# Sorting both halves of a top-1 masked feed forward by expert, in place of dense products over expert groups for the first half, in a two-layer gated kernel on one core

## The chip, the cores and the metric

The program runs on one core of a Trainium2 chip. The metric is the device time in microseconds of one execution; a comparison goes by the median of several runs. The engines of the core are named as the profile names them: PE is TensorE (PEld its weight loads), DVE is VectorE, ACT is ScalarE, POOL is GpSimd, SP is SyncE, which here only issues DMAs.

## What is computed

The input x is 4 x 256 x 256 float32, that is 1024 tokens of 256 features. Four updates of x follow each other; g are gates read from inputs.

```python
x = x + tanh(g_xattn[0]) * attn0(layernorm(x), ctx)        # sim of x, row norm, softmax
x = x + tanh(g_ffn[0])   * ffn0(layernorm(x))              # ternary weight, 32 masks, top 1 of 32
x = x + tanh(g_xattn[1]) * adj1(ctx, layernorm(x))         # top 76 of 256 per row, symmetric part
x = x + tanh(g_ffn[1])   * ffn1(layernorm(x))              # 64 experts, top 8, plus a shared one

def ffn0(x, weight, scale, expert_masks, router_w):        # masks: 32 x 256 x 256
    probs = softmax(x @ router_w.T)
    top1_w, top1_idx = max(probs), argmax(probs)
    w = clip(round(weight / 0.5), -1, 1) * scale[:, None]
    return (x @ (w * expert_masks[top1_idx]).T) * top1_w   # per token
```

## The kernel before

The 1024 tokens are 8 tiles of 128 rows (T = 8), four to a half (HT = 4). X holds the running x, XN its normalised rows, SIM the scores of the second attention, Z scratch. Every engine has its own list of instructions, written out by hand in the order in which it runs; semaphores hold an engine where it needs another's result, and whatever is behind such a wait on that engine waits too.

**The first feed forward.** POOL loads the 32 masks in eight pieces into `m16` (upper half of `gu16`), DVE multiplies each piece by the ternary weight (`mask_weights`, L1643). The two halves of the tokens take different ways. *First half, dense:* `choose(0)` finds each token's expert, `sort_rows` and PE's `group_rows` spread a tile's rows over four groups of eight experts, and PE's `dense(i, ...)` (L1000) multiplies each group with every mask position, 16 products of 16 matmuls; DVE (`dense_rows`, L1468 to L1474), ACT (`started`, `scaled`) and POOL (`add_parts`, `add_rows`) weight the results with `c_mem` and add them up. *Second half, sorted:* `choose(1)`, then PE's `ranks`, `owners`, `owners_of` and DVE's `assign_spares`, `assign_owners`, `assign_slots`, `set_owners` give each token a row number `slot` in a table of 12 x 128 rows, 32 rows per expert and 15 spare blocks for experts with more tokens. POOL's `scatter` (L443) writes the rows to the DRAM tensor `routed_rows`; SP's `load_spares` (L309) copies the weights of each spare block's expert; ACT loads the sorted rows (L719), PE transposes them (`routed_x`, L1018) and multiplies (`experts`, L1039) in six pieces; the results go by DRAM (`expert_rows`, L344) and POOL's `gather` (L451) back to token order.

**The thresholds.** The second attention needs the 76th largest of each row of SIM. DVE finds it with MAX8 and MATCH_REPLACE8 in turn, 19 steps for a tile; `find(n)` takes the next n steps wherever it stands in DVE's list. `adjacency(t)` applies it; `rows_affine`, `rows_sym`, `rows_mix` and `rows_normalise` (L1349) finish a half and hand it to the second feed forward.

**The second feed forward.** 32 pairs of experts and one shared step, for each half of the tokens: PE projects (`project`, L1115), ACT and DVE gate, POOL (`low_step`, L493) makes the low part of a split into two float16, PE multiplies down (L1142). A pair's float32 weights are loaded by SP into one of two stage buffers (`load_pair(q)`, stage q % 2, once pair q - 2 is split), rounded by ACT (`high_half`) and their remainder taken by POOL (`low_half`, L433 and L434). Pairs 0 to 9 are split before the steps begin, the others, four steps ahead, inside the loop of steps n = 2 to 32. At its head PE's list has `shared_step(0)` (L1101), one pair, `prep_wt(0)` (L1091), which needs the token weights, `first_weights` (L1127), the next pair. The token weights come from PE's logits by DVE's `top_find`, ACT's `top_rows` (L755) and DVE's `top_weigh`.

```python
            def load_pair(q):
                s = q % 2
                if q >= 2:
                    sp.wait_ge(lo_ready, q - 1)
```

## Time and profile before

| | us |
|---|---|
| median of 3 runs (407.02 to 409.56) | 408.67 |
| the profiled execution | 407.92 |
| its span on the core | 406.2 |
| PE busy | 384.1 (95%) |
| DVE busy | 283.1 (70%) |
| ACT busy | 184.0 (45%) |
| POOL busy | 162.4 (40%) |

The span runs from the first to the last instruction; what lies around it is 1.7 us. A matmul record's end is modelled, so PE's busy share is no measure of how well it is used. The granted clock of PE is a share of full speed (2.4 GHz): 0.50 is 1.2 GHz.

### The profile page before, as it was taken

The numbers are of one execution on the slowest core, as the hardware profiler recorded it, in microseconds if no ns is written. First come the engines' busy times: TensorE is split into PE (matmuls) and PEld (weight loads), VectorE is DVE, ScalarE is ACT, GpSimd is POOL, SyncE is SP. The second block draws the span as 40 slices with busy tenths as digits, with TensorE's granted clock in tenths as the row PEclk, the third lists the DMA queues.
The fourth block names the chain that finished last, engine by engine and source line by source line (L and its number), as shares of the span: only waits on it lengthen the run. The fifth ranks groups of instructions, "written<-read, shape, count | busy, mean of one in ns | idle before, by whom it ended". The sixth has DMA issues, their size and how long they took to land. (4 is left out here: it accounts for less than half of the span.)

```text
span 406.2 us, 7559 instructions
## 1 busy us (share of the span) xinstructions
PE 384.1 (95%) x2356; PEld 224.0 (55%) x2356; DVE 283.1 (70%) x728; ACT 184.0 (45%) x369; POOL 162.4 (40%) x182
## 2 busy tenths in 40 slices
PE   8989899999789699999999999969999999999995
PEld 2754355444366255656656566545665656656563
DVE  3989888999979568897984775447555545555454
ACT  3477966244166545455455545633333233332331
POOL 6924046849213556995999876220000000000000
PEclk9996999999989899999999999989999999999999
DMA  7799721493212333445456552014121211212211
GB/s 182 124 258 208 105 75 43 126 292 102 81 63 96 116 107 129 143 146 178 144 169 196 157 171 70 7 35 139 61 77 52 77 65 64 77 53 76 71 58 52
DMA packets 46521, 45.13 MB, mean 111 GB/s; under 512 B 6236, under 2 KB 37916, under 8 KB 46494
## 3 DMA queue, kind: packets, MB, share of 16 engines
q1 hardware_dynamic: 35822, 37.69, 30.1%
q0 software_dynamic: 8832, 5.24, 8.4%
q10 hardware_dynamic: 1840, 1.87, 1.6%
q8 instruction: 13, 0.21, 0.2%
q14 instruction: 14, 0.11, 0.1%
HBM read 42.03 MB, written 4.98 MB: 116 GB/s over the span
## 5 line engine op out<-in xcount | busy, mean ns | idle before, releaser
L1115 PE MATMUL bank<-early,gu 128*128 128x512 f16 x768 | 177.7, 381 | 1.3 <-DVE arena L1749 1.3
L1115 PEld LDWEIGHTS bank<-early,gu 128*128 128x128 f16 (+1 forms) x768 | 75.3, 98 | 80.7 <-issue 4.4
L539 ACT ACTIVATE arena<-arena 128x512 f16<-128x512 f32 (+1 forms) x66 | 41.5, 630 | 132.3 <-DVE arena L1765 130.9
L1142 PE MATMUL bank<-dp,arena 128*128 128x256 f16 (+1 forms) x768 | 94.7, 274 | 0.4 <-DVE arena L1775 0.4
L1142 PEld LDWEIGHTS bank<-dp,arena 128*128 128x128 f16 x768 | 75.4, 98 | 22.2 <-DVE arena L1775 0.7
L1749 DVE TENSOR_TENSOR arena<-arena,bank 128x512 f32<-128x512 f32 x64 | 43.9, 686 | 53.5 <-PE bank L1115 38.9
L1000 PE MATMUL bank<-gu,arena 128*128 128x512 f16 x256 | 57.6, 379 | 1.7 <-ACT arena L539 1.7
L493 POOL TENSOR_TENSOR arena<-arena 128x512 f16<-128x512 f32 (+1 forms) x33 | 38.7, 1173 | 39.6 <-ACT arena L539 39.6
L1765 DVE TENSOR_TENSOR arena<-arena,early 128x512 f32<-128x512 f32 x64 | 45.7, 714 | 7.2 <-DVE arena L1749 2.7
L769 ACT ACTIVATE arena<-bank 128x512 f32<-128x512 f32 (+1 forms) x66 | 38.7, 587 | 16.5 <-PE bank L1115 16.5
L433 POOL TENSOR_TENSOR gu<-stage,gu 128x512 f16<-128x512 f32 x32 | 38.4, 1202 | 8.6 <-ACT dp L539 8.6
L1000 PEld LDWEIGHTS bank<-gu,arena 128*128 128x128 f16 x256 | 24.7, 98 | 30.5 <-issue 2.5
L1775 DVE TENSOR_TENSOR arena<-arena 128x512 f16<-128x512 f32 (+1 forms) x33 | 22.8, 692 | 24.8 <-ACT arena L539 24.8
L1272 DVE MAX8 t<-work 128x8 f32<-128x256 f32 x72 | 30.6, 425 | 2.0
L434 POOL TENSOR_TENSOR dp<-stage,dp 128x256 f16<-128x256 f32 x32 | 28.7, 897 | 0.0
L1277 DVE MATCH_REPLACE8 work<-t,work 128x256 f32<-128x256 f32 x64 | 26.1, 408 | 0.0
L426 POOL TENSOR_TENSOR rstd<-var_in,minus_half 128x4 f32<-128x4 f32 x8 | 8.3, 1044 | 40.2 <-DVE var_in L1313 29.4
L539 ACT ACTIVATE arena<-bank 128x512 f16<-128x512 f32 (+2 forms) x28 | 15.6, 590 | 14.5 <-PE bank L1039 8.8
L539 ACT ACTIVATE gu<-stage 128x512 f16<-128x512 f32 x32 | 19.7, 617 | 3.3 <-DMA stage<-in_dp_t 3.2
L827 PE MATMUL bank<-ones 128*128 128x512 f16 x45 | 15.3, 511 | 1.1 <-DVE ones L1647 1.1
L1299 DVE BATCH_NORM_STATS2 bn<-X 128x6 f32<-128x256 f32 x32 | 11.8, 412 | 5.4 <-DMA X<-in_x 5.3
L420 POOL DMA_DIRECT2D gu<-in_masks_t x16 | 12.2, 768 | 3.3 <-DMA X<-in_x 3.3
(199 smaller groups left out, 357.3 us busy)
## 6 DMA issues: line engine op xcount, KB each, us to landing
early<-token_weights SPq DMA_DIRECT2D x126, 128.0 KB, 2.9
stage<-in_gu_t SPq DMA_DIRECT2D x32, 256.0 KB, 2.7
gu<-in_masks_t POOLq DMA_DIRECT2D x16, 256.0 KB, 24.1
stage<-in_dp_t SPq DMA_DIRECT2D x32, 128.0 KB, 3.1
dp<-gu SPq DMA_DIRECT2D x15, 128.0 KB, 2.4
routed_rows<-arena SPq DMA_DIRECT2D x1, 1536.0 KB, 17.8
arena<-routed_rows ACTq DMA_DIRECT2D x4, 384.0 KB, 5.1
expert_rows<-arena SPq DMA_DIRECT2D x6, 256.0 KB, 2.1
```

Source lines behind the costliest of these rows:

```text
L433: nc.gpsimd.tensor_tensor(gu16[:, q, 1, :, :], stage_gu[s], gu16[:, q, 0, :, :], ALU.subtract)
L434: nc.gpsimd.tensor_tensor(dp16[:, q, 1, :], stage_dn[s], dp16[:, q, 0, :], ALU.subtract).then_inc(lo_ready, 1)
L493: nc.gpsimd.tensor_tensor(inter16[0:m, s, 1, :], inter[0:m, s, :], inter16[0:m, s, 0, :], ALU.subtract).then_inc(ilo_ready, 1)
L539: return nc.scalar.activation(dst, src, ACT.Copy, scale=scale)
L769: nc.scalar.activation(silu[0:m, s, :], ps_gate[s][0:m, :], ACT.Silu).then_inc(silu_ready, 1)
L1000: last = mm(dst[:, :], xg[:, k, s, c, g * P:(g + 1) * P], m16[:, c, g * MB + 2 * bp:g * MB + 2 * bp + 2, :].rearrange("p e o -> p (e o)"), ...
L1115: last = mm(dst[:, :], w, x16[:, h, b, c, :], start=(k == 0), stop=(k == 3 * C - 1))
L1142: last = mm(dst, inter16[0:m, s, a, k * P:(k + 1) * P], w, start=(q is None and j == 0 and k % 2 == 0), stop=True, skip_group_check=True)
L1272: last = steps(v.max(t8[:, t, :], src))
L1277: last = steps(v.match_replace(work[:, :], t8[:, t, :], src, NEG))
L1749: v.tensor_tensor(gated[0:m, s, :], silu[0:m, s, :], up, ALU.mult).then_inc(gated_ready, 1)
L1765: v.tensor_tensor(inter[0:m, s, :], gated[0:m, s, :], row, ALU.mult).then_inc(inter_ready, 1)
```

## The change

Both halves of the tokens go the sorted way. `sort_rows`, `members`, `group_rows`, `dense`, `dense_rows`, `started`, `scaled` and `add_parts` are gone. The masks are stored and multiplied expert by expert. There are two sets of spare weights, two `slot` columns, two `expert_rows` tensors, two places for transposed rows; `routed_rows` is used twice. ACT stores the expert results instead of SP; POOL loads the second half's sorted rows. Pairs 0 to 7 are split before the loop of steps, pair 8 in step 4. The diff, cut to what is spoken of:

```diff
+        rows16 = arena[:, 0:4096].rearrange("p (k s n) -> p k s n", k=T, s=2)
+        xs16 = [xs16_0, late[:, 0:2 * ROWS * D].rearrange("p (k n) -> p k n", k=ROWS)]
 # SP
-            for q in range(2, 6):
+            load_pair(2)
+            load_pair(3)
+            load_spares(0)
+            load_pair(4)
+            load_pair(5)
+            load_spares(1)
+            for q in range(6, 8):
                 load_pair(q)
-            load_spares(0, 6)
...
-                if 4 <= n < PAIRS - 6:
+                if 2 <= n < PAIRS - 6:
                     load_pair(6 + n)
 # POOL
+            def load_rows():
+                pool.wait_ge(row_out, 16 * T)
+                pool.wait_ge(sim1_copied, 4)
+                for j in range(3):
+                    nc.gpsimd.dma_start(xs16[1][:, 4 * j:4 * j + 4, :], rows_v[:, 4 * j:4 * j + 4, :]
+                                        ).then_inc(xs_in[1][j], 16)
             rsqrt(1, HT)
+            low_half(0)
             rsqrt(2, HT)
+            low_half(1)
             for t in range(HT):
                 low_rows(t)
+            scatter(0)
+            low_half(2)
+            low_half(3)
...
             for t in range(HT, T):
                 low_rows(t)
-            low_half(2)
-            low_half(3)
-            scatter()
+            scatter(1)
+            load_rows()
+            gather(0)
+            rsqrt(4, HT)
             low_half(4)
-            low_half(5)
...
+            rsqrt(5, HT)
+            for q in range(5, 8):
+                low_half(q)
+            gather(1)
...
-                if n < 2 + HT:
-                    add_rows(n + 2)
-                elif n + 4 < PAIRS:
+                if 4 <= n < 4 + HT:
+                    add_rows(n)
+                if 4 <= n < PAIRS - 4:
                     low_half(n + 4)
 # ACT
             prep_rows(0)
-            expert_rows(PIECES - 1)
-            high_half(8)
-            high_half(9)
+            expert_rows(1, 5)
+            store_rows(1, 5)
+            for q in range(5, 8):
+                high_half(q)
             top_rows(0)
 # PE
+            sim1(1, 0, 1)
+            keep_busy(4, bank[0][:, :])
+            ranks(0)
+            keep_busy(2, bank[0][:, :])
+            owners(0)
+            keep_busy(2, bank[0][:, :])
+            owners_of(0)
+            keep_busy(36, bank[0][:, :])
+            routed_x(0, 0)
+            routed_x(0, 1)
+            experts(0, 0)
+            routed_x(0, 2)
+            experts(0, 1)
+            routed_x(0, 3)
+            router_x((2, 3))
+            experts(0, 2)
+            routed_x(0, 4)
             router(1)
...
+            routed_x(1, 4)
             symmetric(0, 0)
+            symmetric(0, 1)
+            experts(1, 3)
+            routed_x(1, 5)
+            experts(1, 4)
             prep_x3t(0)
-            experts(PIECES - 1)
+            experts(1, 5)
 # DVE
+            def rows_take(t):
+                dve.wait_ge(late_in, 16 * 4)
+                dve.wait_ge(y_in[t], 16)
                 steps.need(rows_mark[0])
+                m = steps(v.scalar_tensor_tensor(Z[:, t, :], Z[:, t, :], wtop[:, t:t + 1], scale_sb[:, :],
+                                                 ALU.mult, ALU.mult))
+                steps.need(m)
+                m = steps(v.tensor_tensor(X[:, t, :], X[:, t, :], Z[:, t, :], ALU.add))
+                steps.need(m)
+                m = steps(moments(X[:, t, :], t))
+                steps.need(m)
+                rows_mark[0] = steps(v.bn_aggr(mv[:, t, :], bn[:, t, :]))
+            find(6)
             choose(1)
+            find(2)
+            assign_spares(1)
...
+            thresholds(HT * need_of - used[0] - 8)
+            rows_take(0)
+            thresholds(2)
...
+            rows_take(3)
+            rows_ask(0)
+            find(2)
             rows_affine(0)
```

**DVE, right behind `choose(0)`.** Before: `grp` is the group of a token, `gu<-ident,grp` the spreading matrices, `picked` and `c_mem` the weights of the group members.

```order
L1427 TENSOR_TENSOR oh<-iota,idxf 128x128 [waits dve_step]
L1434 TENSOR_REDUCE grp<-oh 128x16 [waits dve_step]
L1440 TENSOR_TENSOR gu<-ident,grp 128x512 [waits dve_step]
L1440 TENSOR_TENSOR gu<-ident,grp 128x512
L1446 RECIPROCAL tiny<-tiny 128x4 [waits exp0_ready]
L1448 TENSOR_SCALAR tiny<-tiny,tg 128x4 [waits dve_step]
L1450 TENSOR_TENSOR picked<-oh,tiny 128x128 [waits dve_step]
L1453 TENSOR_REDUCE c_mem<-picked 128x32 [waits dve_step]
L1440 TENSOR_TENSOR gu<-ident,grp 128x512 x2
```

In the changed kernel the same place holds two finder steps and the ranking of the first half, which waits for PE.

```order
L1361 TENSOR_TENSOR oh<-iota,idxf 128x128 [waits dve_step]
L1206 MAX t<-work 128x8 [waits dve_step]
L1211 MATCH_REPLACE work<-t,work 128x256 [waits dve_step]
L1367 TENSOR_SCALAR spares<-full_at,bank 32x15 [waits rank_ready]
L1368 TENSOR_TENSOR picked<-oh,bank 128x128
L1371 TENSOR_REDUCE n_spare<-spares 32x1 [waits dve_step]
L1374 TENSOR_SCALAR n_spare<-ones,n_spare 32x128 [waits dve_step]
L1206 MAX t<-work 128x8 [waits dve_step]
L1380 TENSOR_TENSOR shifted<-shift_e,bank 128x32 [waits prior_ready]
```

What spread the rows over groups has gone; waits for `rank_ready`, `prior_ready` and `owner_ready`, which stood only behind `choose(1)`, now stand behind both.

**ACT, at the head of the second feed forward.** Before: the last expert results (L539 `arena<-bank`), pairs 8 and 9, then `top_rows(0)`.

```order
L539 ACTIVATE arena<-bank 128x512 [waits y_ready]
L539 ACTIVATE gu<-stage 128x512 [waits stage_in0]
L539 ACTIVATE dp<-stage 128x256
L539 ACTIVATE gu<-stage 128x512 [waits stage_in1]
L539 ACTIVATE dp<-stage 128x256
L755 ACTIVATE Z<-lg,tiny 128x64 [waits top_ready]
```

In the changed kernel a store is issued there, and the pairs are 5, 6 and 7.

```order
L506 ACTIVATE arena<-bank 128x512 [waits y_ready]
L641 DMA expert_rows<-arena 128x2x256 [waits y_copied]
L506 ACTIVATE gu<-stage 128x512 [waits stage_in1]
L506 ACTIVATE dp<-stage 128x256
L506 ACTIVATE gu<-stage 128x512 [waits stage_in0]
L506 ACTIVATE dp<-stage 128x256
L506 ACTIVATE gu<-stage 128x512 [waits stage_in1]
L506 ACTIVATE dp<-stage 128x256
L725 ACTIVATE Z<-lg,tiny 128x64 [waits top_ready]
```

Three pairs instead of two stand ahead of `top_rows(0)`, and the first and the third of them use the same stage buffer.

## Rows read from the trace of the kernel before

**Rows 1.** The chain that ended last: start us, us, what (one step of 66).
```profile
281.72 2.70 PE bank L1115 x12
284.42 1.31 PE bank L1142 x12
```

**Rows 2.** Timeline of PE, head of the second feed forward: start us, us, engine line op.
```profile
129.55 1.46 PE L1101 MATMUL bank<-early,shared 128*128 128x512 f16 x6
130.84 2.75 PE L1115 MATMUL bank<-early,gu 128*128 128x512 f16 x12
134.71 0.65 PE L1091 MATMUL bank<-ident,Z 128*65 128x128 f32 x4 [1.11 <-DVE Z L1635]
139.43 4.26 PE L1115 MATMUL bank<-early,gu 128*128 128x512 f16 x12 [1.26 <-DVE arena L1749]
```

**Rows 3.** Timeline of ACT, the same place.
```profile
128.23 0.58 ACT L539 ACTIVATE arena<-bank 128x512 f32<-128x512 f32 x1
131.58 0.35 ACT L755 ACTIVATE Z<-lg,tiny 128x64 f32<-128x64 f32 x1 [1.12 <-DVE tiny L1617]
```

**Rows 4.** Timeline of DVE, from the first half's choice to its hand-over.
```profile
38.17 0.29 DVE L1434 TENSOR_REDUCE grp<-oh 128x16 f16<-128x128 f16 x1
43.93 0.43 DVE L1382 CUSTOM_DVE_ANT_0 Z<-Z,beta_sb 128x256 f32<-128x256 f32 x1
77.53 3.68 DVE L1526 TENSOR_SCALAR tiny<-tiny,tg 128x4 f32<-128x4 f32 x1
87.84 0.43 DVE L1272 MAX8 t<-work 128x8 f32<-128x256 f32 x1
112.10 0.43 DVE L1540 TENSOR_TENSOR Z<-Z,scale_sb 128x256 f32<-128x256 f32 x1
118.78 1.90 DVE L1591 SCALAR_TENSOR_TENSOR X<-SIM,k_mix,Z 128x256 f32<-128x256 f32 x4 [1.89 <-ACT Z L581]
123.84 1.36 DVE L1349 TENSOR_SCALAR XN<-X,mv,rstd 128x256 f32<-128x256 f32 x4
```

**Rows 5.** Groups by line, ten of 17 dense sums: busy us, mean ns | idle.
```profile
L1474 DVE SCALAR_TENSOR_TENSOR Z<-bank,c_mem,Z 128x256 f32<-128x256 f32 x10 | 4.7, 472 | 0.3 <-ACT Z L539 0.2
```

**Rows 6.** Timeline of DVE, the sorted half's ranking, first and last.
```profile
66.78 1.04 DVE L1481 TENSOR_SCALAR spares<-full_at,bank 32x15 f32<-32x15 f32 x1 [0.39 <-PE bank L954]
71.93 0.17 DVE L1519 COPY place<-idxf 128x4 f32<-128x4 f32 x1
```

**Rows 7.** Timelines of POOL and ACT's queue, scatter and load of the sorted rows.
```profile
71.72 1.10 POOL L443 DMA_INDIRECT routed_rows<-gu,slot  x1 [1.56 <-DVE slot L1510]
79.09 2.23 ACTq L719 DMA_DIRECT2D arena<-routed_rows  x4
```

**Rows 8.** Line L719, then line L420 (the masks): time from issue to landing.
```profile
DMA to landing us min/median/max: 3.2/5.1/7.7
...
DMA to landing us min/median/max: 10.8/24.1/28.4
```

**Rows 9.** Timeline of SP's queue, the spare weights.
```profile
88.77 11.74 SPq L309 DMA_DIRECT2D dp<-gu  x9
```

**Rows 10.** The page, DMA issues of a pair: KB each, median us to landing.
```profile
stage<-in_gu_t SPq DMA_DIRECT2D x32, 256.0 KB, 2.7
stage<-in_dp_t SPq DMA_DIRECT2D x32, 128.0 KB, 3.1
```

**Rows 11.** Timeline of POOL: a split at the head, a step's split later.
```profile
129.71 1.16 POOL L433 TENSOR_TENSOR gu<-stage,gu 128x512 f16<-128x512 f32 x1 [6.02 <-ACT dp L539]
130.82 0.67 POOL L434 TENSOR_TENSOR dp<-stage,dp 128x256 f16<-128x256 f32 x1
165.98 1.16 POOL L493 TENSOR_TENSOR arena<-arena 128x512 f16<-128x512 f32 x1 [0.28 <-ACT arena L539]
```

**Rows 12.** Windows: length, busy us of PE, PEld, DVE, ACT, POOL, granted clock, DMA.
```profile
36.00:38.00 2.00, 2.00 (x6) 0.76 (x5) 1.86 (x16) 2.00 (x5) 0.67 (x1) 0.50 1.45 196
140.00:142.00 2.00, 2.00 (x7) 0.64 (x5) 1.08 (x2) 1.23 (x2) 0.71 (x1) 0.50 0.60 200
```

More of the change, by code:

```diff
@@ L720, in _ @@
[L720 to L733 removed]
+            routed_rows(1, 0)
+            routed_rows(1, 1)
@@ L1207, in _ @@
-            for p in range(PIECES - 1):
-                if p == 1:
-                    symmetric(0, 1)
-                experts(p)
-                if p + 2 < PIECES:
-                    routed_x(p + 2)
-            pe.wait_ge(dense_free, len(OWN))
-            keep_busy(12, bank[7][:, :])
+            sim1(1, 0, 1)
[5 more added lines that the diff above has]
+            owners_of(0)
@@ new lines, in _ @@
+            keep_busy(36, bank[0][:, :])
[8 more added lines that the diff above has]
+            routed_x(0, 4)
+            router(1)
+            experts(0, 3, 0)
+            ranks(1)
+            experts(0, 3, 1)
+            routed_x(0, 5)
+            owners(1)
+            experts(0, 4, 0)
+            owners_of(1)
@@ L1215, in _ @@
+            experts(0, 4, 1)
+            experts(0, 5)
+            keep_busy(8, bank[0][:, :])
+            routed_x(1, 0)
+            routed_x(1, 1)
+            experts(1, 0)
+            routed_x(1, 2)
+            experts(1, 1)
+            routed_x(1, 3)
+            experts(1, 2)
+            routed_x(1, 4)
+            symmetric(0, 0)
+            symmetric(0, 1)
+            experts(1, 3)
+            routed_x(1, 5)
+            experts(1, 4)
             prep_x3t(0)
-            experts(PIECES - 1)
+            experts(1, 5)
```

599 lines of the change are left out of this document (210 added, 389 removed).

## The prediction

> **What bounds the kernel now.** The chain that ended last comes first: from 267 us on it is PE almost without a gap, a projection of 2.7 us and a down product of 1.3 us, about 3.9 us a step [rows 1]. There are 66 such steps and no part of the change makes one shorter. So the time is the moment at which the steps get going, plus a constant. PE's timeline around that moment is next [rows 2]: the shared step starts at 129.55, the first pair ends at 133.6, then PE waits for the token weights (134.71) and for the first gated rows (139.43). From there it does not stop. PE's 95% in the page says nothing here; what counts is who is last before 129.55 and who between 133.6 and 139.43.
>
> Before 129.55 it is DVE. It hands the first half over at 123.84 [rows 4], the reader sees finder steps right up to it, and from 38.17 to 123.84 its 85.7 us have few gaps. Between 133.6 and 139.43 it is a round: DVE's `top_find`, ACT's `top_rows` at 131.58 (ACT had waited 1.12 us for it), DVE, PE at 134.71, ACT, DVE, PE [rows 2, 3].
>
> **The dense products (removed).** 256 matmuls leave PE. They lie ahead of DVE's end and their removal shortens nothing by itself: PE already waits for DVE there. What counts is what leaves DVE.
>
> **DVE's list, by difference.** Removed: spreading and member weights, everything from 38.17 to 43.93, 5.8 us [rows 4]; 17 dense sums of 0.47 us, 8.0 us [rows 5]; the wait of 1.9 us for `mix_rows`, which in the changed kernel no longer stands behind expert rows [rows 4]; and 3.4 of the 3.68 us of L1526, a four-element operation that sat beside POOL's splits [rows 4], as the changed place sits beside a scatter. Added: a second ranking; from 66.78 to 72.10 one took 5.3 us with two sums and two finder steps in it, so 3.4 us [rows 5, 6]; four `rows_take` of 1.6 us each (the row at 112.10 starts such a sequence of four operations, here 0.4 each) in place of one of them and three half ones, 3.2 us; two finder steps more before the hand-over and `weights_of_rows(0)`, 1.4 us, a finder step being 0.43 busy and 0.5 with its gap [rows 4]. Sum: -5.8 - 8.0 - 1.9 - 3.4 + 3.4 + 3.2 + 1.4 = -11.1 us.
>
> **DVE's new waits.** (a) The ranking of the first half waits for PE, which has eight float32 products and four fillers ahead of it, at the 1.2 GHz (0.50) that was granted at 36 to 38 us [rows 12]. DVE arrives at 38.2 and two finder steps, 39.2; by an estimate of 6 us for PE's twelve matmuls from 35.5 on, the counts arrive at 41.5: 2.3 us. (b) `choose(1)` waits for the second half's logits, and these now stand in PE's list behind four `routed_x` and three `experts`, which wait for the scattered rows. The slots are there at 41.5 and a ranking of 3.4, 44.9; scatter to first load took 7.4 us (71.72 to 79.09), beside mask products rather 8 [rows 7]; the load lands 3.2 to 5.1 later [rows 8], so 57. Then ACT and PE take turns (a copy of 1.0, one of 0.6 and a store issue of 0.45 a piece, two transposes of x that wait for each other's copy), with PE at 1.2 GHz in part: about 13.5 us, logits at 70.5. DVE gets there at about 66, an estimate from its list (the spare owners, twelve mask products, the second half's softmax and its 13 finder steps, some 21 us of work behind 44.9): 4.5 us. Both ends: no wait at all, or 12 us if PE stays slow throughout. I take 6.8, as the pieces are spaced by ACT in the rows of before too. Hand-over: -11.1 + 6.8 = -4.3 us, at 119.5.
>
> What else must be ready by then: the second half's slots at about 77.5, rows loaded from 85 on, and fifteen spare weights at 1.3 us [rows 9], from 79 to 99, landed by 102. PE wants them behind `symmetric(0, *)`, which waits for the fourth threshold at about 109. So these are hidden with 7 to 10 us to spare.
>
> **The head of the second feed forward.** Before, ACT went from the last expert rows (end 128.81) through pairs 8 and 9, long loaded, to `top_rows` at 131.58: 2.8 us with 1.1 of waiting in it [rows 3]. In the changed list three pairs, 5, 6, 7, stand there, and pair 7 can't be loaded before pair 5 is split, which begins only there. So: store issue 0.5, rounding of pair 5 0.8 (130.46 - 128.81 for two), POOL's split 1.8 [rows 11], issue of the second transfer 0.45 later and landing 3.1 [rows 10], rounding of pair 7 0.8: 7.5 to 7.8 us instead of 2.8. Everything behind `top_rows` (token weights, ACT's silu, the next pair on PE) is later by +4.9 us. Nothing covers it: `top_rows` was already what PE's 134.71 hung on. The bounds: +4.3 if the landing is 2.7, +7 if the queues are busy.
>
> **The clock.** Before, the pair at 139.43 took 4.26 us against 2.75, and the granted clock was 0.50, 1.2 GHz, at 140 to 142 [rows 2, 12], after PE had been mostly idle from 133.6. In the changed kernel this hole grows from 1.1 us to about 6 and the clock will fall earlier, so that the small matmuls of `prep_wt` and `first_weights` (some 3 us, on the path) run at 1.2 GHz too. I take +1.0 (0 to 3). *TensorE: Matmul & The Clock Gate* of the Trainium skill, in HAM oscillation, says that gaps in PE's work bring the lower clock back; by this rule, the trace agrees.
>
> **POOL in steps 4 to 7.** There `add_rows` (two operations, 1.6 us) now comes with a split. At 165.98 POOL had 0.28 us of waiting in a step of 3.6 [rows 11], so it falls behind by about 1 us a step, 4 in all; the low part is used two steps later, 7.8 us [rows 1], and most of that is free. +0.5 (0 to 4). Pair 8 comes four steps ahead of its use, as pair 10 did.
>
> *GPSIMD Engine Reference* of the Trainium skill (Specifications) says that GpSimd and VectorE contend for SBUF interfaces where VectorE runs in a two-port mode or with two SBUF inputs. The row at 77.53 agrees. The mask products have two SBUF inputs and now meet a scatter; by this rule they could be longer. The sum would then be a few tenths higher, no more, as masks and scatter overlap for 7 us only.
>
> **Sum.** -4.3 + 4.9 + 1.0 + 0.5 = +2.1 us. Against the profiled execution (407.92, span 406.2) that is 410.0; this execution was 0.75 under the median, so the median goes from 408.67 to about **410.8**.
>
> **The rivals.**
> *The forecast:* DVE's gain is real, about 4 us, and the stage buffer at the head eats it. Chance 0.48.
> *Faster (0.16):* DVE loses almost nothing to its new waits. Then the hand-over is 11 us earlier: 408.67 - 11.1 + 4.9 + 0.5 = 403. It decides from a gain at the hand-over above 10 us, as less than that leaves under 4 us behind the head. For it speaks that finder steps fill the list between the waits; against it, that `choose(1)` is bound to PE and ACT by program order.
> *Slower, the second half's rows come late (0.16):* POOL loads them through its own queue, and that queue's plain loads, the masks, took 10.8 to 28.4 us to land [rows 8]. Rows scattered by 85, six pieces of 2.4 us: last rows at 99 + landing, against 124.5 by DVE. It decides from a landing above 25 us; at 28.4 the time is 414. Against it: the masks were sixteen transfers on busy engines, here there are three.
> *Slower, POOL doesn't keep up (0.12):* if the buffer of two steps is used up by other things (mix rows, tanh), the 4 us of lag are paid: 414.5.
> *The rest (0.08):* PE slow through the first half's pieces, waits of 12 us: 416.
>
> **The range.** The cases give 403 to 416; with the bounds of the unknown costs 404 to 418 holds 8 in 10. About 1% (4 us) is what a measurement tells from no change: below 404.6 0.18, between 0.50, above 412.8 0.32.
>
> **What would show it.** The changed profile has: the DVE line of `normalise` near 119.5; DVE waiting 3 to 6 us for the logits' bank; ACT waiting 3 to 5 us for DMA `stage` right ahead of `top_rows`; PE waiting 5 to 7 us ahead of `prep_wt`; the second pair on PE near 141, and 3.9 us a step from there. A wait of ACT for `stage` under 1 us would make the head's term wrong; a hand-over before 114 or after 124 would make DVE's sum wrong; PE waits for `ilo_ready` in steps 5 to 10 would speak for POOL.

## The result, and the profile after

The changed kernel took 413.66 us (median of four runs) beside 409.12 for the kernel before: ratio 1.0123, 95% interval 1.0077 to 1.0169. It is slower by 1.2%, some 5 us. Predicted were 410.8 us, 404 to 418.

The executions of one kernel already differ in their first 20 us, and that shifts all that follows: DVE's first request for a root, an early mark, stands at 19.60 us in the profile of before and anywhere from 19.1 to 26.2 in those of the changed kernel and its variants. The inputs are not the reason, for DVE's first operation on x starts at 5.2 to 5.8 us in all of them; PE's first float32 products are what takes longer, here in the second execution of the changed kernel and in the first:
```profile
5.45 1.93 PE L807 MATMUL bank<-early,wk_sb 65*64 65x512 f32 x4
```
```profile
5.50 3.68 PE L807 MATMUL bank<-early,wk_sb 65*64 65x512 f32 x4
```
The first execution, the slowest of the four with 420.7 us, is slow by this alone: its mark stands 6.4 us later, and behind the mark it is no longer than the second. The profile read here is that second execution (414.78 us, span 412.9), in which the mark stands at 19.72, so its times can be laid beside those of before as they are. In the tables every run's times are shifted so that its mark stands at 19.70. *Hand-over* is the first row of `normalise`, *2nd pair* and *3rd pair* are projections of the second feed forward, *31st* the one ahead of `prep_wt(1)`.

| us | hand-over | shared step | `prep_wt` | 2nd pair | 3rd pair | 31st | end |
|---|---|---|---|---|---|---|---|
| before | 123.94 | 129.65 | 134.81 | 139.53 | 145.13 | 261.72 | 406.3 |
| after | 119.03 | 125.95 | 134.72 | 140.03 | 145.03 | 266.53 | 412.9 |
| after, first execution | 119.06 | 125.39 | 135.14 | 140.71 | 146.42 | 266.99 | 412.3 |

From column to column: the hand-over is 4.9 us earlier; from there to `prep_wt` it is 15.7 us for 10.9, so 4.8 are lost, and at the third pair both kernels stand at the same moment (in the first execution the changed one stands 1.3 later). Then, in 28 steps that the forecast had counted at 0.5 us, 4.9 us are lost, 4.0 in the first execution. Seven of the eight traces with this order of work in the steps have 4.0 to 4.2, so 4.0 is the better figure. Another 1.8 (0.7) lie at and behind the second half's preparation. That is no more than scatter: from the 31st projection to the end it is 144.6 to 146.4 us in the traces of all kernels here, and 146.4 in one that has the old kernel's steps (*before, with its share* in the last table).

The way from the hand-over to the shared step is itself no firm figure: it is 6.3 to 8.0 us in traces of kernels whose lists are alike there, while `prep_wt` comes 15.6 to 16.1 us behind the hand-over in all that have the changed kernel's pairs 5, 6 and 7 at the head.

DVE, timeline (start us, us, engine, line, operation; in brackets the idle time before it and who ended it), the places that answer to [rows 4, 6]:
```profile
41.67 0.23 DVE L1367 TENSOR_SCALAR spares<-full_at,bank 32x15 f32<-32x15 f32 x1 [1.42 <-PE bank L928]
44.83 11.07 DVE L1524 TENSOR_TENSOR gu<-gu,tern 128x1024 f16<-128x1024 f16 x12
57.60 0.23 DVE L1414 TENSOR_SCALAR tiny<-tiny,tg 128x4 f32<-128x4 f32 x1
70.70 0.29 DVE L1349 COPY lg<-bank 128x128 f32<-128x128 f32 x1 [2.79 <-PE bank L911]
111.17 1.14 DVE L1462 TENSOR_SCALAR mix<-rstd,k_mix 128x4 f32<-128x4 f32 x1 [0.31 <-POOL rstd L399]
119.05 1.36 DVE L1283 TENSOR_SCALAR XN<-X,mv,rstd 128x256 f32<-128x256 f32 x4
```
The two new waits are there, 1.42 us for the ranks and 2.79 for the logits. `weights_of_rows` takes 0.23 us where it took 3.68 [rows 4]. But twelve mask products take 11.07 us, which the kernel before did in 7.5. The line's own summary says why (durations in ns, smallest, median, largest):
```profile
L1524 DVE TENSOR_TENSOR gu<-gu,tern x16: 677/683/4328, 21.4 to 55.2; 128x1024 f16<-128x1024 f16 x16
```
One product out of sixteen took 4.3 us. It starts at 50.98, and POOL's timeline has at that moment the last scatter and then the two splits of pairs 2 and 3 without a pause:
```profile
50.98 4.33 DVE L1524 TENSOR_TENSOR gu<-gu,tern 128x1024 f16<-128x1024 f16 x1
...
50.26 0.96 POOL L420 DMA_INDIRECT routed_rows<-arena,slot  x1 [0.30 <-issue]
51.25 1.16 POOL L406 TENSOR_TENSOR gu<-stage,gu 128x512 f16<-128x512 f32 x1
52.35 0.67 POOL L407 TENSOR_TENSOR dp<-stage,dp 128x256 f16<-128x256 f32 x1
52.98 1.15 POOL L406 TENSOR_TENSOR gu<-stage,gu 128x512 f16<-128x512 f32 x1
54.09 0.66 POOL L407 TENSOR_TENSOR dp<-stage,dp 128x256 f16<-128x256 f32 x1
```
The product ends at 55.3, half a microsecond behind the last of them. The 3.4 us that [rows 4] shows on L1526 have not gone, they have moved. The affine at 111.17, too, lies beside a split: 1.14 us for its first operation, which takes 0.23 in the kernel before, and 0.59 for the second, 0.16 there.

PE and ACT at the head of the second feed forward, timelines, answering to [rows 2, 3]:
```profile
119.83 1.97 PE L1009 MATMUL bank<-ident,XN 128*128 128x128 f32 x8 [7.02 <-DVE XN L1283]
125.97 1.46 PE L1036 MATMUL bank<-early,shared 128*128 128x512 f16 x6
134.74 0.86 PE L1026 MATMUL bank<-ident,Z 128*65 128x128 f32 x4 [4.72 <-DVE Z L1516]
136.28 1.97 PE L1062 MATMUL bank<-early,ident 65*64 65x512 f32 x2 [0.68 <-ACT early L506]
138.18 2.08 PE L1062 MATMUL bank<-early,pick 65*128 65x512 f32 x2
...
124.72 0.63 ACT L506 ACTIVATE gu<-stage 128x512 f16<-128x512 f32 x1 [0.44 <-ACT arena L506]
130.48 0.63 ACT L506 ACTIVATE gu<-stage 128x512 f16<-128x512 f32 x1 [4.00 <-DMA stage<-in_dp_t]
131.32 0.33 ACT L725 ACTIVATE Z<-lg,tiny 128x64 f32<-128x64 f32 x1
```
ACT waits 4.00 us for pair 7's transfer, PE 4.72 us ahead of `prep_wt`, and what follows runs mostly at the lower of the two clocks, 0.59 in the mean (windows; the seventh figure after the window is the granted clock):
```profile
134.00:140.00 6.00, 4.58 (x8) 1.36 (x9) 1.85 (x6) 3.54 (x5) 3.30 (x4) 0.59 0.40 114
```
And PE's timeline of the steps. In the profile of before no projection or down product waits between the second pair and `prep_wt(1)`; here four do, 3.6 us together:
```profile
180.66 2.75 PE L1050 MATMUL bank<-early,gu 128*128 128x512 f16 x12 [0.33 <-DVE arena L1630]
188.09 1.48 PE L1077 MATMUL bank<-dp,arena 128*128 128x256 f16 x12 [0.69 <-POOL arena L465]
198.68 2.75 PE L1050 MATMUL bank<-early,gu 128*128 128x512 f16 x12 [1.22 <-DVE arena L1630]
204.19 2.75 PE L1050 MATMUL bank<-early,gu 128*128 128x512 f16 x12 [1.37 <-DVE arena L1630]
```

### The profile page after: what moved, and what is told of

Read it like the earlier page. It is cut to its first block and busy times, and to the rows that moved or that the text cites. A ratio compares the mean times of both kernels' runs of the same rounds, so it can differ in the third digit from the quotient of the medians.

```text
span 418.8 us, 7576 instructions
## 1 busy us (share of the span) xinstructions
PE 363.3 (87%) x2360; PEld 217.8 (52%) x2360; DVE 284.0 (68%) x723; ACT 179.0 (43%) x350; POOL 158.4 (38%) x175
## 3 DMA queue, kind: packets, MB, share of 16 engines
q0 software_dynamic: 9648, 7.87, 10.1%
## 5 line engine op out<-in xcount | busy, mean ns | idle before, releaser
L1646 DVE TENSOR_TENSOR arena<-arena,early 128x512 f32<-128x512 f32 x64 | 48.8, 763 | 7.2 <-DVE arena L1630 2.7
L739 ACT ACTIVATE arena<-bank 128x512 f32<-128x512 f32 (+1 forms) x66 | 38.7, 587 | 17.1 <-PE bank L1050 17.1
L798 PE MATMUL bank<-ones 128*128 128x512 f16 x70 | 22.6, 485 | 1.1 <-DVE ones L1528 1.1
L506 ACT ACTIVATE gu<-stage 128x512 f16<-128x512 f32 x32 | 19.7, 616 | 5.4 <-DMA stage<-in_dp_t 4.4
L506 ACT ACTIVATE gu<-bank 128x1024 f16<-128x1024 f16 x12 | 12.0, 1016 | 9.7 <-PE bank L954 9.4
L1233 DVE BATCH_NORM_STATS2 bn<-X 128x6 f32<-128x256 f32 x32 | 11.8, 414 | 4.8 <-DMA X<-in_x 4.5
L506 ACT ACTIVATE arena<-bank 128x512 f32<-128x512 f32 (+1 forms) x18 | 10.7, 593 | 9.8 <-PE bank L978 6.5
L978 PE MATMUL bank<-gu 128*32 128x256 f16 x256 | 11.9, 343 | 3.2 <-ACT gu L506 3.2
L798 PEld LDWEIGHTS bank<-ones 128*128 128x128 f16 x70 | 7.5, 116 | 13.0 <-issue 7.8
```

Of the source, the lines that this page charges most:

```text
L506: return nc.scalar.activation(dst, src, ACT.Copy, scale=scale)
L739: nc.scalar.activation(silu[0:m, s, :], ps_gate[s][0:m, :], ACT.Silu).then_inc(silu_ready, 1)
L798: mm(dst.rearrange("p (a b) -> p a b", a=4), ones16[:, :], ones16[:, None, :].to_broadcast([P, 4, P]), start=True, stop=True)
L1646: v.tensor_tensor(inter[0:m, s, :], gated[0:m, s, :], row, ALU.mult).then_inc(inter_ready, 1)
```

## Experiments

Theory at this point: four separate causes, (1) the stage buffer at the head, (2) POOL and DVE late in the steps, (3) one DVE product held by POOL's splits, (4) DVE's meeting with PE and ACT at the second half's logits. The rivals are that one of them covers for another, or that the second half's rows set the end anyway. Ratios are to the kernel before, measured beside each kernel on the same chip. The moments in the tables are shifted as above.

### The changed kernel again

> The changed kernel once more, unchanged, as the base for the three beside it: about 412.9 us. In the trace: the last mask product of DVE that lies beside POOL's splits of pairs 2 and 3 stretched to 4.4 us where the others take 0.6; DVE waits about 3.5 us for the second half's logits; hand-over (normalise) near 118.5 us; ACT waits about 4.4 us for stage ahead of top_rows; PE waits about 5.7 us ahead of prep_wt; some 4 us lost by PE between steps 10 and 16.

Measured: 418.4 us median of four runs that scatter from 414.8 to 420.9, ratio 1.025 (1.017 to 1.032), above the first measurement. The profile is the one shown above, and each expected figure is near: the long product 4.3 us, the wait for the logits 2.8, the hand-over 119.05, the waits of ACT and PE 4.0 and 4.7, and 4.9 us lost from the third pair to the 31st. Because runs of one kernel can differ by as much as the edits are worth, the following verdicts go by the moments in the traces, one trace a kernel. The times alone would not carry them: beside these four runs the next edits would be worth 5 to 7 us each, beside the first measurement 0 to 2.

### Pair 5 early (cause 1)

```diff
 ACT              high_half(4)
+                 high_half(5)
                  routed_rows(1, 0)
 ...
-                 for q in range(5, 8): high_half(q)
+                 for q in range(6, 8): high_half(q)
                  top_rows(0)
 POOL             low_half(4)
+                 low_half(5)
                  rsqrt(5, HT)
-                 for q in range(5, 8): low_half(q)
+                 for q in range(6, 8): low_half(q)
```

> Pair 5 is rounded and split right behind pair 4, among the expert rows of the second half, so pair 7's transfer is issued ten microseconds before it is wanted. If the stage buffer is what the head pays (theory): ACT's wait of 4.4 us goes, top_rows and prep_wt come 4.8 us earlier, the hole in PE falls from 5.7 to about 1 us, so prep_wt and first_weights run at 2.4 GHz again (-1.9 us), in all -4.8 to -6.7 us, 406 to 408 us. Rival (the round between DVE, ACT and PE is bound by something else that would end just as late, or the steps take the gain back because POOL lags anyway): within 1 us of the base.

Measured: 411.75 us, ratio 1.009 (1.004 to 1.014).

| us | hand-over | shared step | `prep_wt` | 2nd pair | 3rd pair | 31st | end |
|---|---|---|---|---|---|---|---|
| after | 119.03 | 125.95 | 134.72 | 140.03 | 145.03 | 266.53 | 412.9 |
| pair 5 early | 120.56 | 127.34 | 132.24 | 136.96 | 142.38 | 262.99 | 407.9 |

From the shared step to `prep_wt` 4.9 us instead of 8.8 (before: 5.2). PE and ACT of this kernel, timelines:
```profile
134.17 0.65 PE L1028 MATMUL bank<-ident,Z 128*65 128x128 f32 x4 [0.85 <-DVE Z L1518]
135.50 1.07 PE L1064 MATMUL bank<-early,ident 65*64 65x512 f32 x2 [0.68 <-ACT early L507]
138.89 4.08 PE L1052 MATMUL bank<-early,gu 128*128 128x512 f16 x12 [1.26 <-DVE arena L1632]
...
131.02 0.35 ACT L727 ACTIVATE Z<-lg,tiny 128x64 f32<-128x64 f32 x1 [1.10 <-DVE tiny L1500]
```
ACT's wait for `stage` is gone, it waits for DVE again as in [rows 3]. The buffer costs 3.9 us, and the smaller hole gives the higher clock back to `prep_wt` and `first_weights` (0.65 and 1.07 us where they took 0.86 and 1.97), while the second pair is slow as before. The loss in the steps is untouched (120.6 us from the third pair to the 31st against 116.6 before). The theory holds for the head: from the hand-over to `prep_wt` 11.7 us instead of 15.7, to the third pair 21.8 instead of 26.0 (before: 21.2). The time doesn't follow in full, 411.75 where 406 to 408 were expected. A part was paid back at once: the hand-over is 1.5 us later. The logits were already 0.8 us late, and at the affine pair 5's split now holds a further four-element operation (1.19 us for 0.16).

### `add_rows` out of the splits' steps, then the old places for the mixing work (cause 2)

```diff
 ACT, loop        weigh_rows: tiles 4, 5 at n == 2 (was 3), tiles 6, 7 at n == 3 (was 5)
 POOL, loop
-                 if 4 <= n < 4 + HT: add_rows(n)
+                 if 2 <= n < 4: add_rows(2 * n); add_rows(2 * n + 1)
```

> POOL's add_rows of tiles 4 to 7 go two each to steps 2 and 3, where no pair is split, with ACT's scaling of those rows at steps 2 and 3. If POOL's lag in steps 4 to 7 is what costs PE its 4 us between steps 10 and 16 (theory): those waits shrink to under 1 us in sum, time -3 to -4, about 409 us. Rival (the loss comes from mix_rows and tanh_rows on ACT or from DVE's own extra work in these steps, POOL is only near it): within 1 us of the base, and the waits of PE stay.

The second kernel has this and besides:

```diff
 DVE, loop
-                 rows_stats at n = 7..10, rows_ask at 10, rows_affine at 13
+                 rows_stats at n = 5..8,  rows_ask at 8,  rows_affine at 11
 POOL, loop       rsqrt(6) at n == 8 (was 10)
 ACT, loop        tanh_rows(1) at n == 4 (was 6), mix_rows(1) at 12 (was 14)
```

> add_rows two each in steps 2 and 3, as before, and besides DVE's, POOL's and ACT's mixing work of the second half (statistics, their root, affine, mix) two steps earlier, where the kernel before has it. With add_rows alone PE kept one wait of 1.4 us, behind mix_rows at step 14, and lost 2.0 us from step 2 to step 30 against 4 to 5. Theory: the rest is DVE's: steps 9 and 10 now hold four finder steps and the statistics, and step 13 an affine with an adjacency; at the old places PE waits nowhere from step 2 to 30, as in the kernel before: a further -1.5 to -2. Rival (the rest is mix_rows on ACT itself, wherever it stands): the wait of 1.4 us moves to step 12 and stays.

Measured: 411.98 us, ratio 1.007 (1.004 to 1.010), and 410.7 us, ratio 1.002 (0.997 to 1.007).

| us from the 3rd pair to the 31st | |
|---|---|
| before | 116.6 |
| after | 121.5 (120.6 in the first execution, 120.6 with pair 5 early) |
| `add_rows` early | 118.6 |
| and mixing work early | 117.5 |

What PE still waits in these steps, timelines of the one and of the other:
```profile
201.97 2.75 PE L1051 MATMUL bank<-early,gu 128*128 128x512 f16 x12 [1.37 <-DVE arena L1631]
```
```profile
198.60 2.75 PE L1051 MATMUL bank<-early,gu 128*128 128x512 f16 x12 [0.60 <-DVE arena L1631]
```
So POOL's overload in steps 4 to 7 is 2.0 us of the 4.0 (2.9 of the 4.9 in the profile shown), less than the 3 to 4 expected of it alone, and the later places of the statistics and of the mix another 1.1: the statistics now reach into steps 9 and 10, in which DVE has four finder steps instead of three, and the affine and the mix follow them. 0.9 us stay, 0.6 of it as a wait at the step of `mix_rows`: there the rival is right in part. That the two kinds of overload hang together is read from the traces and not tested by itself. POOL's timeline of after shows how the lag builds up,
```profile
154.03 1.16 POOL L465 TENSOR_TENSOR arena<-arena 128x512 f16<-128x512 f32 x1 [2.74 <-ACT arena L506]
...
158.83 1.15 POOL L465 TENSOR_TENSOR arena<-arena 128x512 f16<-128x512 f32 x1
...
163.62 1.15 POOL L465 TENSOR_TENSOR arena<-arena 128x512 f16<-128x512 f32 x1
...
168.93 1.16 POOL L465 TENSOR_TENSOR arena<-arena 128x512 f16<-128x512 f32 x1 [0.28 <-ACT arena L506]
```
4.8 to 5.3 us from one low part to the next where PE needs 3.9: some 3 us of lag after three steps, which use up the lead that ACT, DVE and PE had of each other. The lead doesn't come back in steps in which DVE and POOL are busy for 3.6 to 3.7 of 3.9 us (11.06 and 11.37 of 12 us, at 168 to 180), and the next extra, the affine and the mix at steps 13 and 14, falls on PE directly.

### The splits away from the mask products, then the logits' way shorter (causes 3 and 4)

```diff
 POOL             scatter(0)
-                 low_half(2)
-                 low_half(3)
                  rsqrt(3, HT)
+                 low_half(2)
+                 low_half(3)
```

> POOL's splits of pairs 2 and 3 are moved behind rsqrt(3), away from DVE's mask products and beside finder steps. If POOL's two-input operations are what holds one mask product for 4.4 us (theory): all twelve products take 0.6 to 0.7 us each, DVE's 11.1 us there become 7.3, the hand-over comes 3.7 us earlier and so does the end, about 409 us; if the stall follows the splits to another DVE instruction, that one will be long and the gain smaller. Rival (it is the scatter's indirect transfers that hold DVE): the long product stays, within 0.5 us of the base.

The second kernel has this and besides:

```diff
 PE               experts(0, 0)
+                 router_x((2,))
                  routed_x(0, 2)
                  experts(0, 1)
+                 router_x((3,))
                  routed_x(0, 3)
-                 router_x((2, 3))
+                 router(1)
                  experts(0, 2)
                  routed_x(0, 4)
-                 router(1)
 ACT              the two copies of router_rows(1) behind expert_rows(0, 0) and expert_rows(0, 1)
```

> The splits of pairs 2 and 3 away from the mask products (as in the run before this), and besides the second half's way to its logits made shorter: PE transposes x of tiles 4 and 5 behind the first piece's experts and of 6 and 7 behind the second's, ACT copies them right there, and router(1) stands ahead of the third piece's experts. With the splits alone DVE's products fell from 11.1 to 7.3 us, but its wait for the logits grew from 2.8 to 4.2 us and the hand-over came only 1.4 us earlier. If the meeting of DVE with PE and ACT at these logits is what swallowed the rest (theory): the wait falls under 1 us, the hand-over comes 4 to 5 us earlier than in the changed kernel (near 115 us) and the end 3 to 5 us earlier. Rival (the rows of the second half or their spare weights come too late for a hand-over at 115): DVE gains, but PE then waits for expert rows ahead of prep_logits and the end gains under 2 us.

Measured: 413.46 us, ratio 1.011 (1.008 to 1.014), and 409.54 us, ratio 1.000 (0.995 to 1.006). One of the ten executions behind the second figure took 719.5 us; nothing on record explains it.

| us | logits | hand-over | shared step | 3rd pair | end |
|---|---|---|---|---|---|
| after | 70.68 | 119.03 | 125.95 | 145.03 | 412.9 |
| splits moved | 70.10 | 117.62 | 125.59 | 143.98 | 409.5 |
| and logits earlier | 67.33 | 114.66 | 122.63 | 140.52 | 406.1 |

DVE with the splits moved, timeline:
```profile
44.51 7.31 DVE L1524 TENSOR_TENSOR gu<-gu,tern 128x1024 f16<-128x1024 f16 x12
56.75 0.18 DVE L1326 RECIPROCAL tiny<-tiny 128x4 f32<-128x4 f32 x1 [1.16 <-ACT Z L553]
70.03 0.29 DVE L1349 COPY lg<-bank 128x128 f32<-128x128 f32 x1 [4.21 <-PE bank L911]
```
The products take 7.31 us: it was the splits, not the scatter, whose transfers still lie beside them. But 1.16 us come back as a wait for ACT's exponentials and 1.4 as a longer wait for the logits, and at their new place the splits hold another operation, as was feared: `nmr` (L1341, 128x4) takes 1.00 us at 61.99 where it took 0.15. Of the 3.8 us, 1.4 reach the hand-over. With the second edit the wait is 1.65 us (under 1 was expected), the hand-over 4.4 us earlier than after's and the third pair 4.5; the ratios differ by 0.012 (1.012 and 1.000), 5 us. With the splits alone, the third pair is 1.0 earlier and the median shows nothing. Of 3.8 us ahead of a meeting only the part beyond the slack counts, until the meeting itself is moved. The first theory holds for what held the product, not for what it would bring; the second holds, and its rival (rows too late for 115 us) doesn't: PE still waits 6.9 us for DVE ahead of `prep_x3t`.

### The clock at the head, and the fillers that the change dropped

```diff
 PE               pair_step(0, 0, 0)
+                 keep_busy(18, ps_down[1][:, :])
                  prep_wt(0)
+                 keep_busy(3, ps_down[1][:, :])
                  first_weights(0, I1)
```

> Filler matmuls in the hole of PE at the head: 18 between the first pair and prep_wt (about 3.9 us of the 4.7 that PE waits), 3 behind prep_wt; everything else as in the changed kernel. If it is the lower clock that makes prep_wt, first_weights and the second pair long (theory): the two products of first_weights take 1.1 us each where they took 2.0 and 2.1, the second pair 2.75 where it took 3.7, together -2.7 us, of which DVE's gate step, now last, keeps about 1: time -1.4 to -2.7. Rival (these are long for another reason, as float32 products after a wait): no change in their times, and up to 0.5 us lost.

Measured: 414.6 us median of four runs (410.3 to 419.2), in which no ratio can be read. The trace decides, PE's timeline:
```profile
133.88 0.65 PE L1026 MATMUL bank<-ident,Z 128*65 128x128 f32 x4 [1.76 <-DVE Z L1518]
135.22 1.07 PE L1062 MATMUL bank<-early,ident 65*64 65x512 f32 x2
136.22 1.12 PE L1062 MATMUL bank<-early,pick 65*128 65x512 f32 x2
138.60 2.75 PE L1050 MATMUL bank<-early,gu 128*128 128x512 f16 x12 [1.26 <-DVE arena L1632]
```
All four are at 2.4 GHz (granted clock 1.00 from 129 to 143, where after has 0.76), 3.0 us shorter together than in after, and since PE then waits 1.26 for DVE's gate, from `prep_wt` to the third pair 1.1 us are gained (9.2 against 10.3; the other traces with an unchanged list there have 10.1 to 11.8). The theory holds in kind: it was the clock. The gain is just under its range of 1.4 to 2.7.

```diff
 PE               experts(1, 4)
+                 keep_busy(12, bank[0][:, :])
                  prep_x3t(0)
```

> The twelve filler matmuls that the kernel before has ahead of prep_x3t, and the changed one has not, are put back (2.8 us at 2.4 GHz, 5.2 us at 1.2, in a wait of 7.0 us). Theory: the transposes of XN fall from 1.97 to 1.04 us and the last experts from 1.9 to 1.1, and the shared step comes about 1.2 us closer to DVE's hand-over (5.7 us as before, against 6.9): time -1.2 us, 411.5. Rival (these are not on the path, DVE's lows are): no change.

Measured: 414.8 us, ratio 1.014 (1.006 to 1.022). No gain, a miss:
```profile
113.95 2.76 PE L798 MATMUL bank<-ones 128*128 128x512 f16 x12
119.91 1.76 PE L1009 MATMUL bank<-ident,XN 128*128 128x128 f32 x8 [3.19 <-DVE XN L1284]
```
The fillers ran at once, at 2.4 GHz, and were over 3.2 us before XN came; the transposes took 1.76 instead of 1.04. In the kernel before the same twelve started at 122.68, since PE had been later, and ran past the hand-over, so no wait stood between them and the transposes. How much of a wait may stay uncovered isn't settled here: 1.76 us did no harm in the run before this one, 3.19 did, and so did 2.52 in the last run of the changed kernel below. From hand-over to shared step it is 6.4 us, within the 6.3 to 8.0 of the kernels without these fillers, so nothing that can be told from scatter.

### The second half's rows made late on purpose

```diff
 POOL             scatter(1)
-                 load_rows()
                  gather(0)
+                 load_rows()
```

> POOL gathers the first half's rows (four indirect transfers, about 5.1 us) ahead of loading the second half's scattered rows instead of behind; nothing else differs from the changed kernel. It delays those rows by 5 to 7 us on purpose. If the second half's way through DRAM is hidden with some 7 us to spare (theory; PE still waits 7.0 us for DVE's rows ahead of prep_x3t): PE's wait for the rows grows from 3.6 to about 9 us, its wait for DVE shrinks to 0 to 2 us, the hand-over stays near 119 and the time within 1.5 us of the changed kernel. Rival (the second half's rows are already what the end waits for): 5 us slower.

Measured: 413.35 us (413.2 to 415.0), ratio 1.011 (1.003 to 1.018), the same as after. POOL and PE, timelines:
```profile
88.43 1.00 POOL L437 DMA_INDIRECT Z<-expert_rows,slot  x1 [5.21 <-DMA expert_rows<-arena]
93.19 2.39 POOL L430 DMA_DIRECT2D early<-routed_rows  x3
...
99.43 1.89 PE L954 MATMUL bank<-ident,early 128*128 128x128 f16 x16 [12.27 <-DMA early<-routed_rows]
120.26 1.97 PE L1009 MATMUL bank<-ident,XN 128*128 128x128 f32 x8 [8.31 <-DVE XN L1283]
```
The load is issued at 93.19 where it was at 85.14, PE's wait for the rows grows from 3.6 to 12.3 us (9 were expected), the hand-over stays (118.80), and PE still waits 8.3 us for DVE afterwards (0 to 2 were expected): the pieces themselves go faster than they were spaced, and a wait of 7.8 us that PE had among them for DVE is gone. The load of the sorted rows had landed in 5.9 us through POOL's queue. The second half's way through DRAM is hidden with some 16 us to spare, by an estimate from this run (8.0 of delay taken without loss and 8.3 left).

### Everything together, and the same care for the kernel before

> All edits together on the changed kernel: pair 5 early, splits of pairs 2 and 3 behind rsqrt(3), the logits' way shorter, add_rows and mixing work early, and ACT's first two silu steps ahead of prep_weights (so that the 1.3 us load of its function table and the first gates are done while it waits for PE). If the four causes are separate (theory): -4.8 -1.4 -2.5 -4 -1.3 = -14 us against the changed kernel, near 399 us, below the kernel before. Rival (the causes cover for one another, the gain of one is another's wait): above 404 us.

The next kernel adds the fillers (12 ahead of `prep_x3t`, 4 and 2 around `prep_wt`) and `low_half(4)`, `low_half(5)` ahead of `rsqrt(4)`.

> The changed kernel with all edits of the combined run, and besides: the twelve fillers ahead of prep_x3t, 4 fillers ahead of prep_wt and 2 behind it, and POOL's splits of pairs 4 and 5 ahead of rsqrt(4) instead of beside DVE's affine (whose first operation took 1.13 us there against 0.2). Theory: -0.9 (affine) -1.2 (fillers at x3t) -1.0 (second pair at 2.4 GHz) against the combined run, about 398.5 us. Rival (fillers delay what stands behind them, the splits hold another operation of DVE): 401 to 403 us.

And for comparison the kernel before with what fits it:

```diff
 ACT              top_rows(0)
-                 prep_weights(0)
                  silu_step(0, 1, I1)
                  silu_step(1, 0)
+                 prep_weights(0)
 PE               keep_busy(4, ...) ahead of prep_wt(0), keep_busy(2, ...) behind it
 DVE              mask_weights(7)
-                 weights_of_rows()
                  dense_rows(6, 2)
                  dense_rows(7, 2)
                  find(left // 3)
+                 weights_of_rows()
```

> The kernel before, with those of the edits that fit it: ACT's first two silu steps ahead of prep_weights, 4 filler matmuls ahead of prep_wt and 2 behind it, and weights_of_rows moved from beside POOL's splits of pairs 4 and 5 to behind the first third of the finder steps. Theory: the 3.7 us that one four-element operation of DVE took beside those splits is 0.2 at its new place, if the sums that now lie beside them are not held instead; the hand-over comes up to 3.5 us earlier; the head gains 1.1 (silu) and up to 1.5 (clock): 402.5 to 405 us. Rival: the dense sums beside the splits are held for the same time and only the head's 1 to 2.5 us are gained, 406 to 408 us.

| us | time | ratio to before | hand-over | 2nd pair | 3rd pair | 31st | end |
|---|---|---|---|---|---|---|---|
| before | | 1 | 123.94 | 139.53 | 145.13 | 261.72 | 406.3 |
| before, with its share | 406.9 | 0.995 (0.990 to 0.999) | 124.83 | 139.52 | 143.62 | 260.21 | 406.6 |
| after, all edits | 401.7 | 0.982 (0.972 to 0.992) | 116.47 | 131.75 | 137.23 | 254.77 | 399.4 |
| and fillers, splits | 398.4 | 0.972 (0.965 to 0.980) | 114.08 | 129.34 | 133.44 | 250.25 | 396.5 |

The causes nearly add up: -14 us were expected of the first and its end lies 13.5 us below after's in the traces (1.8 of it behind the 31st projection, where it is scatter), its median 12 us. It holds a fifth edit besides, silu ahead of `prep_weights`, which has no run of its own on the changed kernel: from `prep_wt` to the second pair it is 3.6 us where it was 4.7 with pair 5 early, and in the kernel before 3.8 with this edit and 4.7 without.

The second was expected at 398.5 and came out at 398.4, which is luck in part. Of the three terms, the fillers ahead of `prep_x3t` gave nothing (from hand-over to shared step 6.4 us, 6.3 without them; 1.2 had been expected), those around `prep_wt` 1.4 for 1.0, and the moved splits about 0.6 for 0.9; the logits came 1.8 us earlier with no edit there. It beats both kernels, the one before by 2.8%. Its affine, what the moved splits hold instead, and its head, timelines of DVE and PE:
```profile
94.49 1.80 DVE L1438 SCALAR_TENSOR_TENSOR Z<-Z,tiny,scale_sb 128x256 f32<-128x256 f32 x1
...
107.72 0.23 DVE L1470 TENSOR_SCALAR mix<-rstd,k_mix 128x4 f32<-128x4 f32 x1 [0.30 <-POOL rstd L399]
...
125.73 0.65 PE L1030 MATMUL bank<-ident,Z 128*65 128x128 f32 x4 [0.17 <-DVE Z L1524]
129.53 2.75 PE L1054 MATMUL bank<-early,gu 128*128 128x512 f16 x12
133.63 2.76 PE L1054 MATMUL bank<-early,gu 128*128 128x512 f16 x12
```
The affine's first operation is back at 0.23 us with the splits elsewhere, but one of `rows_take`'s operations takes 1.80 us beside them and 0.47 in the three other tiles. The rival was right there. From the second pair to the third it is 4.1 us, 5.5 in the run without the fillers.

In the kernel before the rival won at the stall:
```profile
91.91 0.52 DVE L1528 TENSOR_SCALAR tiny<-tiny,tg 128x4 f32<-128x4 f32 x1
93.24 0.43 DVE L1301 BATCH_NORM_STATS2 bn<-X 128x6 f32<-128x256 f32 x1 [0.81 <-POOL X L487]
102.81 0.43 DVE L1301 BATCH_NORM_STATS2 bn<-X 128x6 f32<-128x256 f32 x1 [1.20 <-POOL X L487]
```
The four-element operation takes 0.52 us instead of 3.68 and nothing beside the splits is held, but DVE then waits 0.81 and 1.20 for POOL's sums and 0.69 for a dense product, and the hand-over, counted from the slots, is only 0.4 us earlier (52.2 us against 52.6). The 3.7 us had been slack for the most part. Only the head gained, 2.4 us from `prep_wt` to the third pair, and in the profiled execution even that is not to be seen at the end (406.6 against 406.3); the ratio of 0.995 says 2 us, barely clear of none. Measured side by side, the sorted design with all edits and the dense one with its share lie 8.5 us apart in favour of the sorted one. That is not quite a comparison of two designs, as the sorted one's schedule was worked on through several runs and the dense one's in a single one.

## Why the prediction was right, and where it was wrong

The time was in the range and 3 us above the number. At 413.66 it lies in the case above 412.8 (0.32), just beyond the case that had most of the chance (0.50). The mechanism was right: DVE's gain of 4 to 5 us is real, and the stage buffer and the clock at the head eat it. That the number came as near as it did is partly luck, for the sum for DVE came out by errors that balance each other, and the term for the steps was too small by 3.5 us. Point by point:

- **"Steady phase, 3.9 us a step; the time is the moment the steps get going plus a constant."** The first half is right, a step without a wait takes 3.9. The second is the assumption that failed: the constant grew by 4.0 us in the steps (4.9 in the profile shown). At the third pair the changed kernel stands level with the old one or 1.3 us behind it, so most of the difference arises in the steps.
- **DVE's list, -11.1, and waits of 6.8: hand-over at 119.5.** Measured 119.05. The sum is right and its terms are not, so this is luck. The waits were 1.42 for ranks (2.3 expected) and 2.79 for logits (4.5), with 1.1 more at the second ranking's two later meetings. **The term "3.4 of the 3.68 us of L1526" is wrong:** the stall moved to a mask product (3.6 us), because the splits that make it now lie beside the products; and another 1.3 came at the affine. What balanced it was left out: DVE's waits for the dense products and for ACT beside them (1.5 and about 0.7 us) and a 1.0 us operation that is 0.15 now.
- **The rule about GpSimd and VectorE.** The prediction gave it a few tenths, "as masks and scatter overlap for 7 us only". By the Trainium skill (*GPSIMD Engine Reference*, Specifications) the two contend for SBUF interfaces where VectorE has two SBUF inputs; the products have two, and the trace agrees for tensor operations of POOL (4.3 us for one product) and not for its indirect transfers (0.6 each beside them). I had looked at the wrong neighbour.
- **The head, +4.9 (4.3 to 7).** Right: ACT waited 4.0 us for `stage` in the profile shown (4.4 in the first execution); from the hand-over to `prep_wt` it is +4.8 (4.7 to 5.3 over all traces with this head). Taking pair 5 out gives 4.0 back.
- **The clock, +1.0.** Right in kind: `prep_wt` and `first_weights` took 4.9 us instead of 2.85. But the second pair, slow in both kernels, took 0.6 less, and part of it lay beside DVE's gate; with fillers 1.1 us come back.
- **Not seen: the twelve fillers that the diff takes out ahead of `prep_x3t`.** There the transposes take 1.97 us for 1.04 before, and hand-over to shared step 6.3 to 6.9 for 5.7. Putting them back didn't mend it, since they end too early now; what they are worth alone stays open.
- **POOL in steps 4 to 7, +0.5 (0 to 4).** The mis-sized term: 4.0 us in the steps (4.9 in the profile shown), 2.0 of it POOL's lag and 1.1 the mixing work two steps later, which the prediction didn't count. The lag was worked out well (about 1 us a step), and so was the slack of two steps at the low part. What was overlooked, as I read the traces, is that the lead is shared: the same lead carries DVE's affine and ACT's mix at steps 13 and 14, and in the kernel before it was enough for those. The rival "POOL doesn't keep up", 414.5 us at 0.12, is what happened beside the forecast, and 0.12 was too little for it.
- **The second half's rows: hidden.** Right, with some 16 us rather than 7 to 10 to spare; the rival with a landing above 25 us was far off (5.9 us).

## What to carry to other kernels

When a tuned loop is full (DVE and POOL busy for 3.6 to 3.7 of 3.9 us, PE for all of it), an operation that is added to one engine for a few steps isn't free because it is used two steps later: sum all extras that live on the same lead, and look where the next one falls. When an operation disappears that stood in an odd stall, find out who held it before counting it as gained; the holder will take hold of what comes instead. And a double buffer whose reload hangs on a split turns "one more of the same" into a full transfer on the path: count the buffers between the last early item and the first late one.

## What the runs showed of the hardware that I had not expected

- A split by POOL (two operations over 128 rows, 1.2 and 0.7 us) beside a DVE operation with two f16 inputs from SBUF doesn't slow it by a share but holds it to the end of a POOL operation: one product took 4.33 us beside two splits back to back and ended 0.6 us behind the last of their four operations. Finder steps (0.43 and 0.41 us) and sums that read PSUM (0.47) were not held beside such splits. Four-element operations can be: 3.68 us in [rows 4], again to the end of the fourth; 1.14 and 0.59 at the affine against 0.23 and 0.16 in the kernel before, each ending 0.03 to 0.04 us behind a single POOL operation (at 112.27 and 112.90), though POOL went on without a pause; 1.00 for 0.15 at `nmr`. Why some are held for one operation and others for four stays open. Of the places of these splits read here, only one held nothing: beside finder steps and dense sums, in the kernel before with its share.
- The scatter's indirect transfers, issued by POOL beside the same products, left them at 0.6 us each.
- Eighteen fillers kept the granted clock at 1.00 across a wait of 5.8 us of which they covered 4.05. Twelve that ended 3.2 us before the next work left that work at 1.76 us for 1.04. The Trainium skill (*TensorE: Matmul & The Clock Gate*, HAM oscillation) says that gaps bring the lower clock back; the trace agrees.
- The early mark (DVE's first request for a root) differs by up to 7 us between executions, for one and the same kernel from 19.7 to 26.2 us, more than most of the edits are worth. What differs is PE's first float32 products, 1.93 or 3.68 us for four and 3.72 or 6.43 for the sixteen behind them. In two traces with a late mark (21.6 us with pair 5 early, 20.8 in the kernel before with its share) the granted clock was 0.58 and 0.65 from 12 to 20 us, where the others show 1.00; but the one with the latest mark shows 1.00 as well, so the cause stays open.
